# Attention between two tensors on one NeuronCore: the partition moves of the turned probabilities shared by the SyncE and ScalarE queues

## The reference

```python
q = jnp.einsum('bcn,dc->bnd', x1, Wq) + bq
k = jnp.einsum('bcn,dc->bdn', x2, Wk) + bk[:, None]
v = jnp.einsum('bcn,dc->bdn', x2, Wv) + bv[:, None]
attn = jax.nn.softmax(jnp.einsum('bnd,bdm->bnm', q, k), axis=2)
attn_out = jnp.einsum('bcm,bnm->bcn', v, attn)
return attn_out + x1
```

## Time and profile before

| | |
|---|---|
| median of 3 runs | 635.6 us |
| lowest and highest | 634.26 and 635.65 us |
| the profiled execution | 635.0 us, its span 633.2 us |
| PE busy | 629.5 us, 99% of the span |
| DVE, ACT, POOL busy | 442.9, 328.2, 143.3 us |
| TensorE clock granted | full in every slice |

### The profile page before, as it was taken

One profiled execution on the slowest core, in us unless ns is written; L12 is line 12 of the kernel. 1 busy time (PEld: TensorE's weight loads), 2 busy tenths in 40 slices (PEclk: granted clock), 3 DMA queues, 4 the chain that ended last, 5 costly groups with the idle time before them and its releaser, 6 DMA issues.

```text
span 633.2 us, 13435 instructions
## 1 busy us (share of the span) xinstructions
PE 629.5 (99%) x5318; PEld 590.1 (93%) x5318; DVE 442.9 (70%) x511; ACT 328.2 (52%) x430; POOL 143.3 (23%) x115
## 2 busy tenths in 40 slices
PE   9999999999999999999999999999999999999998
PEld 7888899999999999999999999999999999999986
DVE  6995768847778477794777947778568776597351
ACT  6786535735457345474454653555626547265120
POOL 0332200631007400083000830016300353004100
PEclk9999999999999999999999999999999999999999
DMA  8633426963269532776328762287533974345442
GB/s 334 215 133 83 128 84 181 331 143 111 73 176 324 133 126 82 187 285 166 99 83 204 281 159 89 100 227 260 137 93 114 248 243 114 99 132 133 109 145 81
DMA packets 42758, 102.05 MB, mean 161 GB/s; under 512 B 8176, under 2 KB 10224, under 8 KB 42736
## 3 DMA queue, kind: packets, MB, share of 16 engines
q1 hardware_dynamic: 42736, 101.75, 53.4%
HBM read 51.64 MB, written 16.78 MB: 108 GB/s over the span
## 4 chain that ended last, share of the span: by engine, by line
PE 94%; ACT 2%; SPq 2%; DMA 1%; DVE 1%; issue 0%
PE acc_ps L1158 48%; PE acc_ps L1115 23%; PE s_ps L1080 5%; PE s_ps L1228 4%; PE s_ps L1215 3%; PE acc_ps L1178 3%; PE acc_ps L1353 2%; SPq L298 2%; PE acc_ps L1338 1%; PE s_ps L1082 1%; ACT pt_raw L546 1%; PE acc_ps L1190 1%; PE s_ps L1329 1%; DMA pt_raw<-in_front_dram 1%; ACT pt_raw L552 0%; ACT xs_hi L465 0%
## 5 line engine op out<-in xcount | busy, mean ns | idle before, releaser
L1158 PE MATMUL acc_ps<-pt_hi,vt_hi 64*128 64x512 f32 x960 | 201.5, 386 | 0.2 <-DVE pt_lo L727 0.2
L1158 PE MATMUL acc_ps<-pt_lo,vt_hi 64*128 64x512 f32 x960 | 201.3, 386 | 0.0
L1158 PE MATMUL acc_ps<-pt_hi,vt_lo 64*128 64x512 f32 x960 | 201.3, 386 | 0.0
L1158 PEld LDWEIGHTS acc_ps<-pt_hi,vt_hi 64*128 64x128 f32 x960 | 104.3, 184 | 6.5 <-issue 0.8
L1158 PEld LDWEIGHTS acc_ps<-pt_lo,vt_hi 64*128 64x128 f32 x960 | 104.3, 184 | 5.8
L1158 PEld LDWEIGHTS acc_ps<-pt_hi,vt_lo 64*128 64x128 f32 x960 | 104.3, 184 | 5.8
L1115 PE MATMUL acc_ps<-wv_lo,xs_hi 64*128 64x512 f32 x448 | 95.8, 390 | 0.0
L1115 PE MATMUL acc_ps<-wv_hi,xs_hi 64*128 64x512 f32 x448 | 94.9, 386 | 0.0
L433 POOL TENSOR_TENSOR vt_lo<-vt_lo,v_part 128x64 fp32r<-128x64 f32 x56 | 21.0, 380 | 322.1 <-DVE vt_lo L727 322.1
L558 ACT ACTIVATE probs<-s_ps,negmax 128x1024 f32<-128x1024 f32 x56 | 62.5, 1117 | 54.9 <-DVE negmax L814 54.4
L814 DVE TENSOR_REDUCE negmax<-s_ps 128x1 f32<-128x1024 f32 x64 | 76.7, 1210 | 19.7 <-PE s_ps L1082 18.9
(11 more groups left out here) (140 smaller groups left out, 879.2 us busy)
## 6 DMA issues: line engine op xcount, KB each, us to landing
pt_raw<-blocks SPq DMA_DIRECT2D x240, 128.0 KB, 2.3
stage<-in_x_dram SPq DMA_DIRECT2D x32, 512.0 KB, 6.3
o_sb<-in_x_dram SPq DMA_DIRECT2D x64, 256.0 KB, 3.1
out_dram<-o_sb SPq DMA_DIRECT2D x63, 256.0 KB, 2.1
stage<-in_ctx_dram SPq DMA_DIRECT2D x28, 512.0 KB, 9.0
pt_raw<-in_front_dram SPq DMA_DIRECT2D x4, 512.0 KB, 5.7
v_part<-sums SPq DMA_DIRECT2D x56, 32.0 KB, 1.8
stage<-in_front_dram SPq DMA_DIRECT2D x2, 512.0 KB, 7.6
```

What stands on the lines that cost most here:

```text
L1158: mm = nc.tensor.matmul(acc_ps[:, OUT_BANK[group], :], v[rows, m, group * P:(group + 1) * P], p[rows, m, :], start=(swap == 0 and m == 0 a ...
```

## The change

`move` is split by its step number. SP issues the transfers of steps 0 and 1, eight of the sixteen. The other eight, steps 2 and 3, are issued by ACT, by a new function `move` in ACT's block, with the same wait for the four turned tiles in front of them. It is called at the head of `v_phase` (first half) and ahead of `q_cross` (second half; in the last batch ahead of `p_hi`). Sources, destinations, sizes and the count on `s_moved` stay.

```diff
+SP_STEPS = (0, 1)
+ACT_STEPS = (2, 3)
...
                 sp.wait_ge(s_blk, half_of(b, h) * NT + NT)
-                for step in range(NQ):
+                for step in SP_STEPS:
                     for i in range(NQ):
                         j = (i + step) % NQ
                         sp.dma_start(pt_raw[j * Q:(j + 1) * Q, i, :, :],
...
+            def move(b, h):
+
+                act.wait_ge(s_blk, half_of(b, h) * NT + NT)
+                for step in ACT_STEPS:
+                    for i in range(NQ):
+                        j = (i + step) % NQ
+                        nc.scalar.dma_start(pt_raw[j * Q:(j + 1) * Q, i, :, :],
+                                     blocks[i * Q:(i + 1) * Q, j, :, :, :].rearrange("p m t r -> p m (t r)")
+                                     ).then_inc(s_moved, 16)
+
             def v_phase(b):
+                move(b, 0)
                 exp(b, 4)
                 exp(b, 5)
                 for m in range(4):
...
                         round_x1(nb, 3)
+                move(b, 1)
                 if not last:
                     q_cross(nb, first)
```

## The result

The changed kernel takes 675.9 us (median of 6 runs, 672.2 to 678.8) against 634.8 us (634.2 to 635.7). The ratio is 1.064, with a 95% interval of 1.061 to 1.068. The forecast was slower, 640.5 us in a range of 634.2 to 656.0. The direction held; the size was off by more than the whole range. The profiled execution of the changed kernel is the quickest of its six, 672.2 us.

A forecast was written before the change was run, and what follows sets the result against it. PE was taken as the bound, without gaps to close. To the profiled 635.0 us it added seven stalls of 0.78 us (5.5) and took off 0.2, giving 640.3, stated as 640.5 us, range 634.2 to 656.0.

The forecast's parts named there:

- What bounds the kernel: PE, busy 629.5 of 633.2 us with one 0.2 us wait; any added PE wait comes on top of the time.
- The place: First half: ACT's eight issues delay the exponential of tile 4, stalling PE's tile 6 by 0.78 us, seven times, 5.5 us.
- The 4.28 us to spare: First half: time ACT has from 256.98 until the exponential of tile 4 must start, 0.53 us an issue.
- The cost of an issue: Each ACT issue taken at SP's own 0.628 us, so eight take 5.02 us.
- the landing: Last data of a move: about 1 us sooner, not 5, as the engines need some 9.0 us for it.
- The push-back rival: Full DMA engines slow each issue by 0.16 us; first-half stall of 2.05 us, seven times 14.4, 649.2 us; chance 0.20.
- The rival of taking turns: One unit makes descriptors for both queues; first-half stalls of 5.8 us, seven times 40.7, 675.5 us; chance 0.13.
- The clock: PE's clock while it stands still: no row tells it, could make two rivals cost more; nothing in the sum.
- The second half: ACT's eight issues ahead of `q_cross` end 3.6 us before it, so they cost nothing.
- batch 0: Second-half move there: ACT through 0.3 us after `q_cross` now starts; PE's 0.2 us wait booked as a gain.
- SP: Freed of 5.0 us of issue per move; later loads may start sooner; counted as nothing.

The follow-up runs named there:

- e1: Changed kernel with the first half's sixteen transfers all on SP again, only the second half's split: 636.6 us, ratio 1.0024 to the kernel before.
- e2: Changed kernel with the second half's sixteen transfers all on SP again, only the first half's split: 673.4 us, ratio 1.061 to the kernel before.
- e7: Kernel before, all transfers on SP, with seven copies added on ACT ahead of the exponential of tile 4: 671.2 us in one run.
- e6: Changed kernel with only one step, four of sixteen transfers, on ACT in both halves and twelve on SP: 634.3 us, ratio 0.9983 to the kernel before.
- e4: Changed kernel with a quarter of the bytes in each transfer, as many transfers and rows: 644.3 us in one run.
- e3: Changed kernel with all sixteen transfers issued by ACT and none by SP: 723.0 us in one run.
- e9: Changed kernel with half of the bytes in each transfer, as many transfers and rows: 645.1 us in one run.

## Why the prediction was wrong

**What bounds the kernel: right.** PE without gaps, no gain to be had, each us of waiting paid in full. The sum of waits and PE's longer busy time closes to 0.2 us.

**The place: right.** The first half's issues ahead of the exponential of tile 4; e1 and e2 show it, e7 shows it without any transfer. The 4.28 us to spare was nearly right: e6 has no wait at 3.3 us, and in e4 issues of 5.0 and 5.3 us gave waits of 0.63 and 0.92 us, so that some 4.5 us were to spare. Where ACT's issues stood ahead of the exponential, no further wait of PE joined that one in the loop, as forecast; only with all sixteen on ACT (e3) it did.

**The cost of an issue: the step that failed.** I took SP's 0.628 us "as the row nearest to it". As a price of one queue it was right (a median of 0.613 us plus a gap on ACT alone, e3; in two moves each of e4 and e9 ACT's eight took 5.02 us). It was measured, however, with the DMA engines 0.90 busy, and the change doubles the rate at which they are asked. The prediction had the number in hand, since it worked out that the data needs 9.0 us of the engines however it is issued, and used it only for the landing. There it was about right (the last lands 0.7 us sooner, 1 forecast). The 0.90 that it set beside the rule on shared engines was taken with one queue issuing and could not test two. The issue cannot run far ahead of the engines either: sixteen were issued in 7.8 us, with 4.2 us to landing. Two queues that each want 5.0 us for what the engines carry in 9.0 should have been priced between the two and not at the 5.0. Measured were 7.2 to 8.0 us, which made the wait 3.2 us at each move where 0.78 was booked: 22.1 us in all for 5.5. Of the 2.8 us in the move shown (7.81 for 5.02), 0.3 are there at half and quarter bytes too.

**The push-back rival: right in kind, too small.** It took its 0.16 us an issue from HBM loads of 128 rows; it was 0.35 (0.964 for 0.613). Why the loads showed less of it, no run tells. I gave it 0.20 and ended the range with it.

**The rival of taking turns: right in number, wrong in kind.** It said 675.5 us, and 675.9 was measured. Its steps were sixteen issues in 10.05 us and waits of 5.8 us; measured were 7.8 and 3.2, and the rest of its number was made up by PE's longer busy time, most of it the clock's. That the two came to the same time is luck. The Trainium skill's rule behind it ("Perfetto Trace Analysis", section "DMA Instruction — HWDGE (DVE, Sync)"), that sequencers lock a shared descriptor unit, does not show here as a lock for the whole issue: the first issues of both take their 0.53 us side by side, and at half the bytes all but one or two a move keep their own pace. A shorter hold would fit the 0.3 us a move that one queue loses there. Had only the time been looked at, this rule would have passed for confirmed.

**The clock: named, put at nothing in the sum.** At the wait, the granted clock fell to its lower level in six of the seven moves. PE worked 22.4 us at the lower level in all (6.2 of them behind the second wait, 3.0 to 3.4 behind each of five others), and half of that, 11.2 us, is what it lost: the greater part of the 12.7 us of longer busy time. A smaller part comes with the waits themselves: at full clock throughout, e4 and e9 still have PE busy 1.9 and 2.2 us longer over eight and nine waits. With the issue cost set right and the clock left out, the forecast would still have been some 13 us short.

**The second half: right but for batch 0.** Its cover of 3.6 us held in the loop, even with issues of 0.97 us. In batch 0 I had ACT late by 0.3 us; it was late by some 3, as the issues took 7.86 us, and the 0.2 us wait became 2.4 instead of nothing (2.2 in e1, and none in e2, where SP issues all sixteen there). e6, where ACT is through in 3.5 us, has the gain that I had booked.

**SP: as forecast,** no gain from its freed 5 us, and only 2.6 us of it were freed.

## What to carry to other kernels

An engine that computes pays for each transfer that it issues with time in its own order, and the price is not the issue time of a lone queue: where the DMA engines are near full already, the issue is held towards their pace. So price it between the issue time of a lone queue (5.0 us here) and all the bytes over the rate that the engines show (9.0; 7.2 to 8.0 was measured), and compare it with the time until the next instruction on that engine is wanted; four of sixteen transfers fit here and were free, eight cost 6%. A second queue is of use where one queue's issue, and not the data, sets the pace. And when a forecast time is met, compare its steps: here a wrong mechanism gave the right time.

## What was not expected of the hardware

- Issues on two queues at once were not slowed at the first transfer of each (0.53 us), and at half or a quarter of the bytes only by 0.3 us a move (median 0.61 us). With full rows of 4 KB they went to a median of 0.93 to 0.97 us, when the transfers between partition groups of 32 ran at 222 GB/s in all.
- PE's clock after a wait is not settled by the length of the wait. In the changed kernel it stayed full after a wait of 2.95 us, and it was at its lower level after one of 3.56 us and also after one of 2.82 us, the last of the seven (in this order, the stretches behind them):

```profile
113.00:117.00 4.00, 3.46 (x32) 2.94 (x34) 3.27 (x7) 2.56 (x6) 0.48 (x2) 1.00 0.98 240
195.00:199.00 4.00, 4.00 (x20) 3.27 (x22) 3.82 (x6) 1.82 (x4) 0.65 (x2) 0.50 0.95 269
607.54:610.54 3.00, 3.00 (x14) 2.49 (x16) 2.79 (x6) 2.02 (x4) 0.29 (x1) 0.50 0.86 238
```

  Nor is it the same from one execution to the next. In batch 0 of e1 there is a single wait of 2.2 us, and the stretch around it has a mean clock of 0.83:

```profile
70.00:80.00 10.00, 8.00 (x56) 7.84 (x58) 9.09 (x10) 4.95 (x5) 0.00 (x0) 0.83 0.07 27
```

  That execution is the slowest of e1's ten (638.5 us) and the only one with a mean clock under 1.000; the other nine took 636.2 to 637.3 us. What decides it stays open. For a forecast, a wait of 2 to 3 us may or may not bring the clock down, and its price is uncertain by that much.
